# A decoder layer on one core: feed-forward tiles behind the state sums, the first convolution tap on ScalarE, and another order in the last chunk and in routing

## The reference

```python
# 1. Mamba block on the layer-normed tokens, one sequence of 2048
xz = x @ in_proj_w.T;  u, z = split(xz)                 # 2 x 512 channels
u = silu(causal_dwconv(u, conv_w, conv_b))              # 4 taps a channel
dt, B, C = split(u @ x_proj_w.T)                        # 16 + 16 + 16
delta = softplus(dt @ dt_proj_w.T + dt_proj_b)
h = exp(delta * A) * h + delta * u * B                  # 16 states a channel, over time
y = (sum_n h * C + u * D) * silu(z)
h1 = rmsnorm(residual + y @ out_proj_w.T)
x = x + rmsnorm(h1 + gelu(h1 @ ffn_w1.T + b1) @ ffn_w2.T + b2)
# 2. cross attention: 16 heads of 16, 1601 keys
x = x + softmax(q @ k.T / 4) @ v @ Wo + bo
# 3. soft mixture of 8 experts with 128 slots each
logits = norm(x) @ slots.T                              # 2048 x 1024
x = x + combine(softmax over slots, experts(softmax over tokens @ norm(x)))
```

## Time and profile before

| what | value |
|---|---|
| median of 3 runs | 1473.03 us |
| profiled execution, its time | 1476.31 us |
| its span, first to last instruction | 1474.5 us |
| busy: TensorE / VectorE / ScalarE / GpSimd | 1297.6 / 755.9 / 931.9 / 398.6 us |
| mean granted TensorE clock | 0.939 |

### The profile page before, as it was taken

The page is one execution under the profiler, slowest core; times in us unless marked ns, Lnnn a source line. Parts: engine busy times, 40 slices in busy tenths (PEclk is TensorE's granted clock), DMA queues, the critical chain, the costliest instruction groups (busy, mean ns, idle before and its releaser), DMA issues.

```text
span 1474.5 us, 14685 instructions
## 1 busy us (share of the span) xinstructions
PE 1297.6 (88%) x5523; PEld 632.3 (43%) x5523; DVE 755.9 (51%) x849; ACT 931.9 (63%) x1320; POOL 398.6 (27%) x309
## 2 busy tenths in 40 slices
PE   5678996987968796997879999999999987999999
PEld 1233442434433353354522223323323233588988
DVE  4899979998899979983231000100100126561011
ACT  3847645575537744742269999999999963661310
POOL 1656755565446656650000000000000000000000
PEclk9789888999989998998979999999999999999999
DMA  5434564243224423456442000000000000011701
GB/s 165 143 111 128 189 206 186 86 144 115 85 86 132 134 86 136 136 207 150 98 112 72 0 1 1 1 1 1 1 1 0 1 0 29 4 83 41 330 16 43
DMA packets 42870, 127.60 MB, mean 87 GB/s; under 512 B 6086, under 2 KB 21254, under 8 KB 39399
## 3 DMA queue, kind: packets, MB, share of 16 engines
q1 hardware_dynamic: 42796, 126.62, 26.7%
HBM read 109.51 MB, written 17.09 MB: 86 GB/s over the span
## 4 chain that ended last, share of the span: by engine, by line
PE 53%; DVE 23%; ACT 14%; issue 7%; DMA 2%; POOL 1%; SPq 0%; DVEq 0%; ACTq 0%
PE ps L1951 11%; DVE ps L1140 11%; PE ps L1939 10%; ACT arena L971 6%; DVE arena L1151 4%; PE ps L2022 4%; PE ps L1804 4%; PE ps L2097 4%; PE ps L2140 4%; PE ps L1749 3%; PE ps L1554 3%; ACT ps L766 2%; PE ps L2115 2%; PE ps L1793 2%; DVE arena L1085 2%
## 5 line engine op out<-in xcount | busy, mean ns | idle before, releaser
L971 ACT ACTIVATE arena<-ps,bound 128x1024 f32<-128x1024 f32 (+1 forms) x416 | 425.5, 1120 | 11.6 <-PE ps L1951 3.6
L592 POOL TENSOR_TENSOR arena<-arena 128x1024 f32<-128x1024 f32 x128 | 301.9, 2358 | 251.6 <-DVE arena L1151 190.8
L1140 DVE TENSOR_TENSOR_SCAN ps<-ps,arena 128x1024 f32<-128x1024 f32 x128 | 300.5, 2347 | 10.4 <-ACT ps L766 5.5
L1749 PE MATMUL ps<-arena,ident 128*128 128x512 f32 x512 | 243.0, 621 | 0.3 <-DVE arena L1151 0.3
L1939 PE MATMUL ps<-arena 97*128 97x512 bf16 (+1 forms) x832 | 215.0, 385 | 19.4 <-ACT arena L971 14.2
L1951 PE MATMUL ps<-arena 128*32 128x512 f32 (+1 forms) x1664 | 208.2, 603 | 0.5 <-ACT arena L971 0.5
L766 ACT ACTIVATE ps<-arena 128x512 f32<-128x512 f32 x256 | 166.3, 682 | 61.9 <-DVE arena L1151 58.0
L579 POOL TENSOR_TENSOR rstd<-ve,mhalf 128x4 f32<-128x4 f32 (+2 forms) x21 | 25.0, 1192 | 575.6 <-DVE ve L1414 481.7
L1151 DVE TENSOR_TENSOR arena<-ps,arena 128x1024 f32<-128x1024 f32 x128 | 155.8, 1217 | 13.3 <-DMA arena<-bc_scratch 7.5
L1441 DVE COPY arena<-ps 128x512 f32<-128x512 f32 x16 | 11.1, 691 | 288.9 <-PE ps L1951 288.9
L1749 PEld LDWEIGHTS ps<-arena,ident 128*128 128x128 f32 x512 | 100.4, 200 | 127.4 <-issue 120.9
(11 more groups left out here) (181 smaller groups left out, 1383.6 us busy)
## 6 DMA issues: line engine op xcount, KB each, us to landing
arena<-bc_scratch SPq DMA_DIRECT2D x128, 512.0 KB, 4.4
arena<-in_mw SPq DMA_DIRECT2D x16, 1024.0 KB, 9.3
qx_scratch<-arena SPq DMA_DIRECT2D x48, 128.0 KB, 2.4
arena<-qx_scratch SPq DMA_DIRECT2D x4, 1536.0 KB
arena<-kx_scratch SPq DMA_DIRECT2D x1, 4803.0 KB
kx_scratch<-arena SPq DMA_DIRECT2D x36, 128.0 KB, 4.2
arena<-vx_scratch SPq DMA_DIRECT2D x1, 3328.0 KB
vx_scratch<-arena SPq DMA_DIRECT2D x6, 512.0 KB, 2.9
```

Of the source, the lines that this page charges most:

```text
L592: pool.tensor_tensor(dbu[:, w % DR], du[:, DP * p:DP * p + DP], over(bg[:, w // BG % 2, n % BG], DP), ALU.mult).then_inc(S["dbu_ready"], 1)
L971: act.activation(flat(prob[v % 3][0:n, 2 * h:2 * h + 2]), ps[0:n, 2 * (r % 3):2 * (r % 3) + 2, :].rearrange("p a b -> p (a b)"), ACT.Exp, ...
L1140: dve.tensor_tensor_scan(decay_banks(w), decay_banks(w), flat(dbu[:, w % DR]), carry[:, DP * p, n:n + 1], ALU.mult, ALU.add).then_inc(S["s ...
L1749: last = mm(bank(x), ident[:, :], state(2 * j + s)[:, x], start=False, stop=(j % HP == HP - 1 and (j in SUMMED or s == 1)))
```

## The change

It has five parts.

1. *Convolution.* ScalarE, having copied a channel block out of PSUM, writes the first tap with bias from the same PSUM block (Identity with scale and bias). VectorE keeps the other three taps.
2. *Seams.* At the end of a chunk only tile 0 of the feed-forward's second layer stands in step 31, tile 1 in step 0 and tiles 2 and 3 in step 2, behind the last sums. What waits for them (second residual, mean, norm, step sizes of the second half) stands one or two steps later in chunk 2 too, as it did in chunk 3.
3. *Last chunk.* Residuals and the first norm stand earlier, pieces of queries and feed-forward one step later, and only tiles 0 and 1 of chunk 2 remain in the loop (steps 27 and 29).
4. *Behind the loop.* The output projection of the last chunk goes to banks 2 and 3 and its norm to a place of its own (`h1_tail`), and neither waits for chunk 2's residual; tiles 2 and 3 of chunk 2 follow it. The first norm of chunk 3 stands ahead of the second norm of chunk 2.
5. *Routing.* `normed_tokens(t + 2)` goes to the head of VectorE's step. `combined(t)` gives one group of turned weights for tiles 8 to 11 and two for 12 to 15, the first between the halves of the logits, and 4 groups instead of 8 are left behind the loop.

```diff
+PAIRED = TAIL + CT
+INSIDE = TT - TAIL + TT - PAIRED
+        h1_tail = Stack(zs_at + DK * C).take(CT, DM)
...
+        def normed_of(c):
+            return h1_tail if c == NC - 1 else h1
+        def projected(c, b):
+            return bank(2 + b) if c == NC - 1 else work(b)
+        def h1_bank(c, k):
+            return bank(4 + k) if c == NC - 1 else work(k)
...
+        def combined(t):
+            if t < TAIL:
+                return ()
+            return (t - TAIL,) if t < PAIRED else (2 * t - PAIRED - TAIL, 2 * t - PAIRED - TAIL + 1)
...
@@ scalar
-                act.activation(upad[:, d, TAPS - 1:TAPS - 1 + C], work(d), ACT.Copy).then_inc(S["u_raw"], 1)
+                act.activation(upad[:, d, TAPS - 1:TAPS - 1 + C], work(d), ACT.Copy)
+                act.activation(channels_of(c, d // DP)[:, d % DP], work(d), ACT.Identity, bias=ch("conv_b")[:, d:d + 1],
+                               scale=ch("conv_w", TAPS)[:, d, TAPS - 1:TAPS]).then_inc(S["u_raw"], 1)
...
-            second_squares(NC - 2)
             first_squares(NC - 1)
             turned_h1(NC - 1)
+            second_squares(NC - 2)
...
@@ vector
-                for step, j in enumerate(reversed(range(TAPS))):
-                    if step == 0:
-                        dve.tensor_scalar(out, upad[:, d, j:j + C], conv_w[:, d, j:j + 1],
-                                          ch("conv_b")[:, d:d + 1], ALU.mult, ALU.add).then_inc(S["conv_step"], 1)
...
-                if i == 17 - 3 * late and c:
+                if i == 17 - 5 * last and c:
                     first_norm(c - 1)
...
             gated(NC - 1, 1)
-            second_residual(NC - 2)
-            second_mean(NC - 2)
+            second_residual(NC - 2, 0)
             for b in range(2):
                 first_residual(NC - 1, b)
+            first_mean(NC - 1)
+            first_norm(NC - 1)
+            second_residual(NC - 2, 1)
+            second_mean(NC - 2)
             second_norm(NC - 2)
             mamba_out(NC - 2)
-            first_mean(NC - 1)
-            dve.wait_ge(S["x1_ready"], NC - 1)
-            first_norm(NC - 1)
...
             for t in range(TT):
+                if t + 2 < TT:
+                    normed_tokens(t + 2, t + 3)
...
-                if t + 2 < TT:
-                    normed_tokens(t + 2, t + 3)
...
@@ tensor
-                    if i < 2 and c >= 2:
-                        ffn_out(c - 2, 2 + i, 0)
-                        ffn_out(c - 2, 2 + i, 1)
+                    if i == 0 and c >= 2:
+                        ffn_out(c - 2, 1)
+                    if i == 2 and c >= 2:
+                        ffn_out(c - 2, 2)
+                        ffn_out(c - 2, 3)
...
-            pe.wait_ge(S["r_ready"], 2 * (NC - 1))
             for i in range(CT):
                 out_project(NC - 1, i)
+            ffn_out(NC - 2, 2)
+            ffn_out(NC - 2, 3)
             turn_h1(NC - 1)
...
-                logits(t)
+                logits(t, 0)
+                for e in combined(t)[:-1]:
+                    turn_combine(e)
+                logits(t, 1)
                 if t < TAIL:
                     tail_piece(t)
-                else:
-                    turn_combine(t - TAIL)
+                for e in combined(t)[-1:]:
+                    turn_combine(e)
```

More of the change, by code:

```diff
@@ L903, in _ @@
                         rank_b_c(c + 1)
-                    if i == (20 if more else 16) and c:
+                    if i == (20 if more else 17) and c:
                         turned_h1(c - 1)
@@ L912, in _ @@
                         hidden(c - 1, i - 24)
-                    if i in (17, 19, 21, 24) and not more:
-                        hidden(c - 1, 2 * (17, 19, 21, 24).index(i))
+                    if i in (18, 20, 22, 25) and not more:
+                        hidden(c - 1, 2 * (18, 20, 22, 25).index(i))
                     if c == 0:
@@ L1233, in between @@
                         normed_input(1)
-                late = 0 if more else 1
+                late = 1 if c >= 2 else 0
+                last = 0 if more else 1
                 if i == 2 and c:
@@ L1259, in between @@
                     conv_keep(c + 1)
-                if i in (12 - 4 * late, 13 - 4 * late) and c:
-                    first_residual(c - 1, i - 12 + 4 * late)
-                if i == 14 - 3 * late and c:
+                if i in (12, 13) and c and more:
+                    first_residual(c - 1, i - 12)
+                if i == 8 and not more:
+                    first_residual(c - 1, 0)
+                    first_residual(c - 1, 1)
+                if i == 14 - 4 * last and c:
                     first_mean(c - 1)
@@ L1334, in _ @@
             dve.wait_ge(S["h1_ready"], NC * CT)
-            second_residual(NC - 1)
+            for b in range(2):
+                second_residual(NC - 1, b)
             second_mean(NC - 1)
@@ L1763, in out_project @@
                 for d in range(DB):
-                    last = mm(work(i // 2)[:, part(i % 2)], zs[:, c % 2, d, tok(i)], wout[:, d],
+                    last = mm(projected(c, i // 2)[:, part(i % 2)], zs[:, c % 2, d, tok(i)], wout[:, d],
                               start=(d == 0), stop=(d == DB - 1))
@@ L1822, in _ @@
                     w = c * NU + i
-                    if i == 3 and more:
+                    if i == 3 and c < 2:
                         step_input(c, 1)
-                    if i == (19 if more else 15) and c:
+                    if i == 19 and c and more:
                         turn_h1(c - 1)
```

184 lines of the change are left out of this document (96 added, 88 removed).

## The result

The changed kernel takes 1417.76 us (median of four runs), the kernel before 1470.18 us: a ratio of 0.9637 (0.9594 to 0.9679). One of the four, at a granted clock of 0.823, took 1537.59 us and is left out of the ratio and of all that follows; the other three lie at 1416.43 to 1419.05, with a median of 1416.46. In a second comparison it took 1420.85 against 1471.6, ratio 0.9663 (0.9637 to 0.9689). Forecast were 1421 and 1408 to 1441. The profiled execution took 1416.46 (span 1414.7), that of before 1476.31. Either kernel was profiled a second time: 1419.68 (`after_again`) and 1472.54 (`before_again`).

A forecast was written before the change was run, and what follows sets the result against it. VectorE was taken to bound the scan loop, with waits for TensorE's order there and TensorE waiting for VectorE in routing. Terms summed to 55.7 us off the profiled 1476.3, a median of 1417.3, taken as 1421; range 1408 to 1441.

The forecast's parts named there:

- Convolution, 8.2: First taps leaving VectorE: 6.5 us from twelve in the loop, 1.7 from four ahead of it; bounds 3 and 8.6.
- the 0.7 which the prediction named as a sign of being wrong: First tap on ScalarE: Identity expected at 0.687 us like L846; above 0.7 would make the prediction wrong.
- Ahead of the loop, 1.7 of it: Four first taps before the loop: 4 x 0.54 us less work, begun some 0.5 later.
- Starts of chunks 2 and 3, 8.8 and 7.8: Reordered seams cut `gated` waits: 8.8 us at chunk 2, net of two decay waits (2.5 together); 7.8 at chunk 3.
- The gain up to chunk 2: Stretch from the first scan to `gated` at chunk 2: forecast to gain 13.3 us.
- The loop's end, 11.8: `gated` wait behind the loop falls from 13.62 to 1.8 us; bounds 6 and 12.
- chunk 3's decays, 2.3: VectorE's waits for decays in the last chunk fall from 4.8 to 2.5 us; bounds -2 and 4.8.
- TensorE, 7 us ahead, has half a pair of sums left, 1.8: Loop's end: TensorE could end at 643.7, VectorE at 650.5, so the last `gated` wait is 1.8 us.
- Behind the loop, 1.2: After the last `gated`: out_project from T+1.3, hidden ends at T+32.8 instead of T+34.0; 1.2 us gained, bounds -4 and 2.
- Routing, 16.1 and -0.5: Tiles 0 to 7 gain 16.1 us: waits 14.7, faster logits 2.5, less 1.1; tiles 12 to 15 and end -0.5.
- the third rival's case: Transposes not counting as activity, the clock falls in routing from tile 12: some 23 us, 1444; chance 0.08.
- the 4 us held back for unseen waits: Allowance over the summed 1417.3, giving 1421, for new waits not placed and crowded places in ScalarE's queue.

The follow-up runs named there:

- the two kernels: Changed kernel with the first tap back on VectorE: 1424.79 us; kernel before with the first tap alone moved to ScalarE: 1464.76 us (ratio 0.9945).
- copies_early: Changed kernel with ScalarE's copies of the turned query and turned h1 one step earlier in the last chunk: 1419.31 us, ratio 0.965.
- tap_back: Changed kernel with the convolution's first tap back on VectorE: 1424.79 us, ratio 0.9681.
- seams_back: Changed kernel with only TensorE's old order at the seams (tiles 0, 1 in steps 30, 31; 2, 3 in steps 0, 1): 1436.94 us, ratio 0.9759.
- tile_out: Changed kernel with tile 1 of chunk 2 moved behind the loop too: 1419.43 us, ratio 0.9631.
- two kernels with earlier and faster matmuls: Changed kernel with ScalarE's turned query and h1 copies one step earlier: 1419.31 us; with repeated transposes in TensorE's idle, turned h1 one step later: 1421.36 us.

## Why the prediction was right, and where it was not

- *Convolution, 8.2.* Right within what the runs tell: 5.7 and 8.1 by the two kernels, 2.3 for 2.15 in chunk 2. One reading under it was wrong. L846 was taken for the same form, but it has a bias per partition alone, and the new Identity a scale as well. For 128x512 out of PSUM the rows have 0.592 us with neither (the Copy, L719), 0.687 with one and 0.773 with both. That is above the 0.7 which the prediction named as a sign of being wrong, and it cost nothing that can be read.
- *Ahead of the loop, 1.7 of it.* The first scan starts at 45.3 to 45.7 in five profiles with the tap on ScalarE and at 48.7 to 49.1 in six, though the program is the same up to it. TensorE's timeline has it. After:

```profile
26.19 3.61 PE L1734 MATMUL ps<-arena 128*48 128x512 f32 x8 [3.39 <-ACT arena L726]
```

And in `copies_early`:

```profile
26.83 6.48 PE L1734 MATMUL ps<-arena 128*48 128x512 f32 x8 [3.39 <-ACT arena L726]
```

The same eight products behind the same idle, at one level or the other. With the tap on VectorE there are two levels too. Before, and then `tap_back`:

```profile
32.15 3.77 PE L1732 MATMUL ps<-arena 16*128 16x512 f32 x4 [0.68 <-ACT arena L717]
...
31.74 1.98 PE L1759 MATMUL ps<-arena 16*128 16x512 f32 x4 [0.68 <-ACT arena L735]
```

The first scan starts at 48.7 in the one and at 46.8 in the other. At the higher level in both the gain is 1.1 to 1.5, near the 1.7; the 3.2 in the table sets the lower level before against the higher after.
- *Starts of chunks 2 and 3, 8.8 and 7.8.* Right, in size and mechanism; the two new waits for decays stood where they were placed, 2.83 together for 2.5. In chunk 3 none came. `seams_back` gives both waits of `gated` back.
- *The gain up to chunk 2* was 20.8 for 13.3. What was missing is no step of the change: 6.3 us of waits for rows of C (7.5 to 3.0) and for ScalarE's L744 (1.8 to 0), behind TensorE's clock in chunk 0. The step that failed is the silent one, that chunk 0 stays as it was but for its taps. It does in the program, but not from one execution to the next: the second profiles give 16.8.
- *The loop's end, 11.8, and chunk 3's decays, 2.3.* Mis-sized. The step that failed is "TensorE, 7 us ahead, has half a pair of sums left, 1.8": work and waits were summed over the whole chunk, while step 19 brings both engines level and only the 59.5 us behind it count, of which TensorE works 57.85. It is the later engine there; 8.9 came of 11.8. The sum also left TensorE no waits in that chunk; it has 15.2 us of them, most ahead of step 19. `tile_out` bears this out: with a tile less behind step 19 the 1.8 came, as 2.08. Waits for decays were 5.2 in the last chunk, not 2.5, though in other steps: ScalarE, in order, has them behind GELUs and copies, before which it waits for TensorE's products (2.15 and 1.03 us at 574.76 and 583.35), so part of them is TensorE's lateness once more. That they are nothing else is not shown. How far the last chunk fell short is not sure either, 4.7 in the first profiles and 8.0 in the second, since before took 144.15 us there in one and 140.76 in the other.
- *Behind the loop, 1.2.* Right: 1.0; out_project stood at T+1.3, hidden from T+18.6 to T+32.7.
- *Routing, 16.1 and -0.5.* Right in the sum (16.0 for 15.6). Of its parts `normed_tokens` is worth 17.5 and the pairs cost 1.1: the exps lie 11.1 behind the last logits, not 10.0. Steps last 4.1 us, 5.4 at tiles 6 and 7, then 4.5 and from tile 12 on 5.2, forecast as 4.3, 4.5 and 5.4. The clock stayed at 1.00 from tile 9 on, so the third rival's case did not come.
- *The sum.* 55.7 stands against 59.9 between the first profiles and 52.9 between the second, and against medians that differ by 53.7 in the first comparison and 50.8 in the second. The profile of before lay at 1476.3 and that of after at 1416.5, each at one end of its runs. In the first profiles a surplus in chunk 0 and ahead of the loop (9.0), most of it the level of the clock, and a shortfall in the last chunk (4.7) offset each other: that much of the closeness is luck. In the second profiles, which lie nearer to the medians, the sum falls 2.8 short, and the 4 us held back for unseen waits cover that.

## What to carry to other kernels

Where two engines meet at a fixed step, sum work and waits from the last such meeting, not over the loop: slack ahead of it buys next to nothing, as two kernels with earlier and faster matmuls showed (1.1 us at most). Put what the next engine waits for ahead of work that only fills, and check that it was waiting for order and not for amount; at the seams it was order (15 us), at the loop's end amount. When terms come from one profile of each kernel, profile each twice, and sort by the level of the clock before reading a gain: here a stretch with the same program moved by 3 us, and another by 6.

## What was not expected of the hardware

- After the same idle of 3.39 us the same eight matmuls took 3.61 us in one execution and 6.48 in another: which level of the clock TensorE is at behind an idle is not fixed by the program.
- Four products of the values tiles took 2.08 us behind an idle of 1.27 us in one execution and 1.13 behind one of 1.28 in another.
- 4.53 us of transposes and 2.53 us of idle left the clock up, where 1.91 us of transposes and 4.83 us of idle did not.
- An operand that differs by partition has a price on ScalarE: 0.592 us without, 0.687 with a bias, 0.773 with scale and bias, each on 128x512 from PSUM.
